# A selective state-space layer with a mixture of experts: nine row states in place of eight, three of the row products summed by accumulating DMAs, and a new order of work

## The reference

```python
proj = einsum('blh,he->bel', xn, W_in); hidden, gate = split(proj, 2)      # E = 512 channels each
hidden = silu(causal_conv4(hidden) + conv_bias)
dt, Bm, Cm = split(hidden^T @ W_x, [128, 144])                             # N = 16 states
dts = softplus(dt @ W_dt + b_dt); A = -exp(A_log)
state[n] = exp(dts * A[n]) * state[n] + dts * hidden * Bm[n]               # over the 256 tokens
scan_out = sum over n of state[n] * Cm[n]
ssm = ((scan_out + hidden * D) * silu(gate))^T @ W_out
# moe: softmax router over 32 experts, top 8 renormalised, sum of w_e * (silu(x@wg) * (x@wu)) @ wd, inner width 96
```

## Time and profile before

| | us |
|---|---|
| median of 3 runs | 1346.49 |
| runs | 1344.55 to 1347.49 |
| profiled execution, device time | 1342.44 |
| its span (first to last instruction) | 1340.6 |
| PE busy / PEld busy | 1301.6 / 1219.6 |
| DVE busy | 1239.6 |
| ACT busy | 1213.2 |
| POOL busy | 1233.9 |

### The profile page before, as it was taken

One profiled execution on the slowest core, in us unless ns is written; L12 is line 12 of the kernel. 1 busy time (PEld: TensorE's weight loads), 2 busy tenths in 40 slices (PEclk: granted clock), 3 DMA queues, 4 the chain that ended last, 5 costly groups with the idle time before them and its releaser, 6 DMA issues.

```text
span 1340.6 us, 26644 instructions
## 1 busy us (share of the span) xinstructions
PE 1301.6 (97%) x9222; PEld 1219.6 (91%) x9222; DVE 1239.6 (92%) x1644; ACT 1213.2 (90%) x2111; POOL 1233.9 (92%) x674
## 2 busy tenths in 40 slices
PE   6899999999999999999999999999999999999998
PEld 5889999999999999999999999999999899999987
DVE  3799999999999999999999999999999999999997
ACT  5879999999999999999999999999999899999984
POOL 2999999999999989999999999989999999999996
PEclk9999999999999999999999999999999999999999
DMA  7543443544444344443544444344443534434342
GB/s 193 160 144 118 143 120 115 152 115 132 139 127 135 112 136 127 139 120 118 149 120 126 136 128 138 114 132 131 139 122 116 148 114 134 139 113 142 109 146 80
DMA packets 189399, 174.95 MB, mean 130 GB/s; under 512 B 43185, under 2 KB 172241, under 8 KB 189265
## 3 DMA queue, kind: packets, MB, share of 16 engines
q1 hardware_dynamic: 150864, 121.86, 30.5%
q10 hardware_dynamic: 38400, 51.40, 13.6%
HBM read 167.92 MB, written 5.24 MB: 129 GB/s over the span
## 4 chain that ended last, share of the span: by engine, by line
POOL 27%; issue 21%; ACT 19%; DVE 18%; PE 12%; DMA 2%; ACTq 1%; SPq 0%; DVEq 0%; POOLq 0%
POOL state L571 14%; POOL moe L586 6%; ACT decay L657 5%; PE pair_ps L1003 5%; ACT L657 5%; ACT L665 4%; DVE state L878 4%; PE out_ps L1138 3%; POOL state L580 3%; DVE dt L865 3%; DVE u L891 2%; DVE decay L878 2%; DVE u L919 2%; ACT moe L665 2%; DVE moe L898 2%
## 5 line engine op out<-in xcount | busy, mean ns | idle before, releaser
L571 POOL TENSOR_TENSOR state<-du,b_rep 128x1024 f32<-128x1024 f32 x256 | 611.7, 2395 | 61.1 <-DVE u L891 59.3
L878 DVE TENSOR_TENSOR_SCAN state<-decay,state 128x512 f32<-128x512 f32 x448 | 534.2, 1212 | 21.1 <-ACT decay L657 16.4
L657 ACT ACTIVATE decay<-dt,neg_a 128x255 f32<-128x255 f32 x1024 | 436.7, 465 | 37.7 <-DVE state L878 19.0
L1138 PE MATMUL out_ps<-w_down,moe 128*128 128x256 f32 x1536 | 355.9, 381 | 3.1 <-POOL moe L586 1.9
L1138 PEld LDWEIGHTS out_ps<-w_down,moe 128*128 128x128 f32 x1536 | 282.5, 190 | 38.6 <-issue 4.1
L586 POOL TENSOR_TENSOR moe<-moe,rw_rep 128x512 f32<-128x512 f32 x192 | 249.3, 1309 | 8.7 <-DVE moe L898 7.3
L580 POOL TENSOR_TENSOR state<-state,c_rep 128x1024 f32<-128x1024 f32 x96 | 244.1, 2543 | 1.6 <-DVE state L878 1.6
L1003 PE MATMUL pair_ps<-xnT_hi,w_gate_hi 128*128 128x256 f32 x768 | 228.9, 298 | 3.2 <-DVE moe L898 3.2
L1003 PE MATMUL pair_ps<-xnT_hi,w_up_hi 128*128 128x256 f32 x768 | 225.7, 294 | 2.8 <-ACT moe L665 1.9
L657 ACT ACT_TABLE_LOAD x171 | 219.4, 1283 | 2.5
L1003 PE MATMUL pair_ps<-xnT_lo,w_gate_hi 128*128 128x256 f32 x768 | 216.4, 282 | 0.0
(11 more groups left out here) (149 smaller groups left out, 2252.5 us busy)
## 6 DMA issues: line engine op xcount, KB each, us to landing
w_down<-in_L_ffn_w_down_dram SPq DMA_DIRECT2D x384, 128.0 KB, 2.9
b_rep<-b_dram ACTq DMA_DIRECT2D x128, 256.0 KB, 3.3
rw_rep<-rw_dram SPq DMA_DIRECT2D x256, 96.0 KB, 2.7
c_rep<-b_dram ACTq DMA_DIRECT2D x128, 128.0 KB, 3.3
rw_rep<-rw_dram SPq DMA_DIRECT2D x256, 64.0 KB, 2.6
rw_rep<-rw_dram SPq DMA_DIRECT2D x256, 32.0 KB, 2.6
x_in<-L_attn_input_states_dram SPq DMA_DIRECT2D x16, 256.0 KB, 3.8
res<-L_attn_input_states_dram SPq DMA_DIRECT2D x16, 256.0 KB, 3.1
```

The lines of the kernel that those rows point to most:

```text
L571: pool.tensor_tensor(state[:, n % STATES, :, :], du2[:, q, :, :], b_rep[:, n // BCH % 2, n % BCH, :][:, None, :].broadcast_to([P, ET, T]), ...
L657: last = act.activation(decay[:, h, j, 1:T], dt[:, q, e, 1:T], ACT.Exp, scale=neg_a[:, e, n:n + 1])
L878: dve.tensor_tensor_scan(a if n in ROWS_BY_VECTOR else x, a, x, 0.0, ALU.mult, ALU.add).then_inc(scanned, 1)
L1138: last = pe.matmul(out_ps[:, c, :], moe[:, p % RING, j, c * P:(c + 1) * P], w_down[:, p % RING, j, :], start=(p == 0 and j == 0 and c == 0 ...
```

## The change

Row states are now (2, 4, 5, 6, 7, 9, 11, 12, 14). 5, 7 and 9 are VectorE's own; 2, 4, 6, 11, 12 and 14 are multiplied on GpSimd; of these, 11, 12 and 14 are added to `u2` not by VectorE but by a DMA that GpSimd issues with an add (`move_row`; 512 KB from SBUF to SBUF each). Seven states are left by turn. All tables of slots are new, those for the first and the last block too; ACT's table loads come out as 284 instead of 347, counted in the order of the two kernels.

```diff
-    BY_ROW = [n for n in range(NS) if n in ((2, 4, 5, 6, 8, 9, 10, 12))]
+    BY_ROW = [n for n in range(NS) if n in ((2, 4, 5, 6, 7, 9, 11, 12, 14))]
...
-    ROW_ADD_AT = [[42, 54, [45, 47], 70, 80, [76, 79], 106, 116], ...
+    ROW_ADD_AT = [[39, 53, [40, 46], 71, [61, 61], [75, 79], 93, 102, 118], ...
...
-    ROWS_BY_VECTOR = [n for n in BY_ROW if n in ((5, 9))]
+    ROWS_BY_VECTOR = [n for n in BY_ROW if n in ((5, 7, 9))]
+    ROWS_BY_DMA = [n for n in BY_ROW if n in ((11, 12, 14))]
...
+        def moved_at(i, n):
+
+            return (i * len(ROWS_BY_DMA) + ROWS_BY_DMA.index(n) + 1) * 16
...
+            elif ROW_SUMS[k] in ROWS_BY_DMA:
+                eng.wait_ge(row_moved, moved_at(i, ROW_SUMS[k]))
...
+                    elif before in ROWS_BY_DMA:
+                        pool.wait_ge(row_moved, moved_at(at, before))
...
+            def move_row(i, q, n):
+
+                wait_summed(pool, i, ROW_SUMS.index(n) - 1)
+                row_multiplied(pool, i, n)
+                pool.dma_start(u2[:, q, :, :], state[:, n % STATES, :, :], accum_op=ALU.add).then_inc(row_moved, 16)
...
             def gated(i, q):
 
+                pool.wait_ge(gate_read, 2 * i + 2)
                 pool.wait_ge(y_summed, 2 * i + 2)
...
+                for n, at in zip(BY_ROW, ROW_ADD_AT[s]):
+                    if n in ROWS_BY_DMA and a == at:
+                        move_row(i, q, n)
...
-                    if n not in ROWS_BY_VECTOR and a == at:
+                    if n not in ROWS_BY_VECTOR and n not in ROWS_BY_DMA and a == at:
                         add_row(i, q, n)
```

More of the change, by code:

```diff
@@ L102, in build @@
-    SCALAR_ALONE = [{'conv_silu': -74, 'router_exp': -94, 'softplus': -29, 'first_state': 4, 'skip': -9, 'normed': -123, 'share': -45},
-                    {'conv_silu': -73, 'router_exp': -84, 'softplus': -20, 'first_state': 7, 'skip': 23, 'normed': -122, 'share': -62},
-                    {'conv_silu': -73, 'router_exp': -77, 'softplus': -17, 'first_state': 13, 'skip': 4, 'normed': -123, 'share': -62}]
-    GATE_SILU_AT = [[54, 64], [63, 68], [74, 189]]
-    MUL_AT = [[-10, 13, 41, 55, 60, 67, 79, 85, 108, 112, 118, 124],
-              [14, 23, 41, 46, 59, 63, 79, 92, 107, 108, 127, 129],
-              [28, 34, 51, 54, 67, 72, 82, 82, 100, 117, 179, 190]]
@@ new lines, in build @@
+    OUT_AT = [[33, 43, 63, 71, 78, 84, 100, 119, 128, 128, 141, 141],
+              [39, 39, 57, 68, 70, 86, 103, 118, 118, 120, 141, 141],
+              [39, 65, 77, 108, 108, 174, 185, 188, 224, 235, 237, 253]]
+    TURN_AT = [[[8, 9], [9, 10], [22, 37], [74, 83], [103, 106], [122, 122], [130, 130]],
+               [[21, 22], [29, 29], [49, 49], [80, 82], [105, 105], [115, 116], [121, 129]],
+               [[14, 23], [24, 30], [37, 57], [84, 85], [154, 157], [182, 191], [211, 211]]]
+    TURN_Y_AT, PROJECT_AT = [[141, 141], [141, 142], [233, 233]], [163, 164, 254]
@@ new lines, in build @@
+    SCALAR_FRONT = [{'xnT': -116, 'hid0': -115, 'hid1': -114, 'weightsT': -6, 'low': -83, 'lowT': -82, 'dt0': -66, 'dt1': -51},
+                    {'xnT': -115, 'hid0': -102, 'hid1': -89, 'weightsT': -54, 'low': -44, 'lowT': -40, 'dt0': -30, 'dt1': -21},
+                    {'xnT': -110, 'hid0': -102, 'hid1': -90, 'weightsT': -49, 'low': -40, 'lowT': -33, 'dt0': -29, 'dt1': -22}]
+    SCALAR_ALONE = [{'conv_silu': -104, 'router_exp': -111, 'softplus': -24, 'first_state': 8, 'skip': 5, 'normed': -119, 'share': -93},
+                    {'conv_silu': -74, 'router_exp': -73, 'softplus': -17, 'first_state': 22, 'skip': 33, 'normed': -118, 'share': -60},
+                    {'conv_silu': -60, 'router_exp': -73, 'softplus': -18, 'first_state': 13, 'skip': 2, 'normed': -118, 'share': -59}]
@@ new lines, in build @@
+    GATE_SILU_AT = [[54, 71], [61, 71], [55, 151]]
+    MUL_AT = [[-22, -20, 30, 41, 56, 62, 77, 94, 108, 111, 128, 129],
+              [19, 31, 46, 48, 61, 63, 74, 77, 105, 109, 128, 130],
+              [18, 19, 47, 48, 66, 78, 93, 102, 124, 176, 213, 222]]
+    ADD_AT = [[[23, 30], [35, 68], [72, 97], [111, 114], [116, 126], [127, 132]],
+              [[28, 34], [69, 69], [92, 102], [105, 107], [118, 128], [128, 133]],
+              [[20, 29], [59, 61], [89, 89], [92, 119], [158, 170], [184, 209]]]
@@ new lines, in build @@
+    SUM_AT = [[136, 141], [141, 143], [240, 244]]
+    WEIGH_AT = [[19, 25, 29, 35, 51, 53, 84, 91, 101, 104, 122, 126],
+                [27, 30, 33, 41, 57, 65, 72, 85, 102, 105, 123, 124],
+                [26, 38, 51, 63, 63, 89, 97, 99, 131, 147, 237, 237]]
+    ROW_MUL_AT = [[21, 35, [40, 45], 51, [60, 61], [74, 79], 89, 100, 107], [21, 33, [44, 45], 45, [60, 62], [73, 76], 90, 95, 108], [20, 33, [43, 44], 55, [57, 62], [72, 78], 90, 125, 202]]
+    POOL_ALONE = [{'rstd': -103, 'step_input': -19, 'gated': 140, 'select': -47},
+                  {'rstd': -126, 'step_input': -22, 'gated': 139, 'select': -68},
+                  {'rstd': -122, 'step_input': -21, 'gated': 249, 'select': -60}]
@@ L138, in build @@
-    SPLIT_SCALAR_AT = [-115, -104, -102, -86, -73, -68, -51, -44, -41, -30, -28, -13, -7, -3, 0, 0, 10, 18]
-    SPLIT_POOL_AT = [-116, -112, -96, -69, -50, -2, 7, 11, 12]
+    WARM_AT = [[-73, 19], [8, 31], [22, 22]]
+    SPLIT_VECTOR_AT = [-108, -50, -50, -35, -34, -11, 6, 7, 16]
+    SPLIT_SCALAR_AT = [-121, -113, -112, -110, -88, -85, -83, -79, -50, -27, -23, -4, -4, -4, 1, 8, 8, 18]
+    SPLIT_POOL_AT = [-94, -25, -24, -21, -21, 5, 8, 9, 13]
     def pieces(p):
@@ L371, in row_at @@
         def row_at(i, n):
-            of = [k for k in BY_ROW if k not in ROWS_BY_VECTOR]
+            of = [k for k in BY_ROW if k not in ROWS_BY_VECTOR and k not in ROWS_BY_DMA]
             return i * len(of) + of.index(n) + 1
+        def moved_at(i, n):
+            return (i * len(ROWS_BY_DMA) + ROWS_BY_DMA.index(n) + 1) * 16
         def read_a(i, name):
```

54 lines of the change are left out of this document (16 added, 38 removed).

## The result

The changed kernel is slower: 1352.55 us (median of 5, 1351.1 to 1353.42) against 1345.43 us (median of 5, 1341.42 to 1347.49), a ratio of 1.0054 [1.0036, 1.0071]. The forecast was 1332.5, faster. Its direction was wrong. Its range, 1319 to 1358, held the time by luck: it reached that far up only for rival A, and what brought the time there was in good part the last block, which the forecast took to get 0.9 us shorter.

What follows compares the result with a forecast made beforehand. TensorE was taken as the bound; eight transposes fewer cut the period from 80.41 to 79.54 us, 13.9 us over 16 blocks: 1342.4 to 1328.5, plus 4.1 for the median, about 1332.5. The 80% range was 1319 to 1358.

Steps and rivals of the forecast that it cites:

- rival A: GpSimd becomes the bound through DMA issue and landing times; slower, 1368, at the upper ends 1403; chance 0.23.
- TensorE sets the pace, and the three others are close behind it.: Middle block: TensorE needs about 78 of 80.4 us, the largest need; DVE 3.5, POOL 4.8 and ACT 4.8 us away.
- buy nothing: VectorE, middle block: net -3.4 us, 76.85 to about 73.5, gains nothing by itself since VectorE isn't the bound.
- The 4.2 us of waiting for row adds are slack of an engine that is early: GpSimd's waits for VectorE's row adds, 4.2 us a block, were slack and counted as nothing.
- Behind the change no full add is left in that part: Where rows 10 and 12 were added, GpSimd's two lengthened operations lose their excess: 2.0 us, 75.6 to 73.6.
- c: Time one DMA issue holds GpSimd, put at 1.3 us between bounds 0.33 and 2.40; three with draining cost 4.2 us.
- The landing: Time until an adding DMA lands, put at 5 us; cost 0.2 us a block on GpSimd, ends 0 and 3.1.
- GpSimd's need: GpSimd's work and stalls in a middle block after the change: 78.0 us, 1.5 us under the forecast period of 79.54.
- The last landing is far from VectorE's `y_sum`: Block end: over 10 us of other work lie between, so the end of the block doesn't wait for it.
- C: Rival: half of TensorE's 2 us of stops a block also go, another 1.0 a block; time 1317, chance 0.15.
- rival B: No net gain: GpSimd's need between 79.5 and 80.4, or state 8's decays waiting for row 7; 1344 to 1349, chance 0.12.
- Start and last block, "unchanged": First and last block and the tables of the start were counted as unchanged.

Runs made afterwards that it cites:

- e1: Kernel before with 8 matmuls of pair 6's gate unit left out, 0.94 us less TensorE a block in its first half: 1345.65 us, ratio 1.0006.
- e5: Changed kernel with the same 8 matmuls of pair 6's gate unit left out, 0.94 us of TensorE a block: 1356.39 us, ratio 1.0095 to the kernel before.
- e11: Changed kernel without the three adding DMAs and their sums, and with 8 matmuls fewer a block: 1321.77 us, ratio 0.9837 to the kernel before.
- f1: Changed kernel with GpSimd's weight product of pair 9, late in the block, cut from 512 to 32 columns: 1342.56 us, ratio 0.9986 to the kernel before.
- e2: Changed kernel without the three adding DMAs and their sums; nobody waits for a landing: 1322.6 us, ratio 0.984 to the kernel before.
- f4: Kernel before with GpSimd's weight product of pair 9, late in the block, cut from 512 to 32 columns: 1338.38 us, ratio 0.996.
- e10: Changed kernel with pair 6's 8 matmuls left out and GpSimd's weight product of pair 6 cut to 32 columns: 1354.76 us, ratio 1.0085 to the kernel before.

## Why the prediction was wrong

**The step that failed: "TensorE sets the pace, and the three others are close behind it."** It was read off a budget over a whole block, 78 needed of 80.4. e1, e5 and e11 say no, in the kernel before, in the changed one, and without the DMAs: 0.94 us less of TensorE gave 0.07 us or nothing, cut in the first half. Every engine had 2 to 5 us of room over the block, and the period came from stretches in which one or two had none. (TensorE as one of several pacers late in a block of the kernel before is not excluded.) From this step it followed that VectorE's 4.5 us "buy nothing", that up to 1.5 us on GpSimd are free, and that the sum is the eight transposes. In its place the runs show that late in the block GpSimd counts (0.73 us of the period for 1.0 us of its work, f1), and there the DMAs stand: +2.03 us a block, against -1.91 for the rest of the change (e2, without three row sums). The forecast had 0 and -0.87.

**"The 4.2 us of waiting for row adds are slack of an engine that is early": wrong.** f4 takes one microsecond off GpSimd late in a block of the kernel before and shortens the period by 0.47. An engine can wait early in a block and be the pace late in it.

**"Behind the change no full add is left in that part": right, and only half of the matter.** GpSimd's long operations are gone (step input 3.34 to 2.64; adds on VectorE 1.55 us in the mean, now 1.24). But the three full adds that stay, and row 7, all lie in the first half, which they fill to 99%.

**The DMAs.** The issue was put at c = 1.3 with 0.1 for draining the product; it reads 0.94, of which 0.6 to 0.7 hold the queue, and the draining is 0.55. The reason given for the middle value, that GpSimd computes and ScalarE does not, is none: ScalarE is busy 75.6 us a block. Three cost 3.2 us of the queue instead of 4.2. The landing was put at 5: 5.4 in the median, with waits of 1.8 us in five blocks, 0.4 each instead of 0.2. GpSimd's need, forecast 78.0, is 77.45 busy and these waits. Between DMA 12 and the wait for its landing lie 8.2 us (682.60 to 690.82) and not over 9, which is still enough. All in all well sized, and compared with the wrong thing: a whole period instead of the second half. "The last landing is far from VectorE's `y_sum`" is right for the middle blocks and wrong for the last one, where `y_sum` stands 2.3 us for it.

**The others.** TensorE 79.94 to 78.92 a block (forecast -0.87), VectorE 76.85 to 72.35 (-3.4; the rest is the shorter adds), ScalarE 75.58 to 69.98 (forecast -4.4), table loads 284: right or nearly so as work, and without the effect on the period that C hoped for.

**The rivals.** Rival A named the mechanism, the DMAs' time on GpSimd, and the side. Its decision point was wrong: it asked for c over 2.1 us, since it too measured GpSimd against the whole block, and so its 1368 was too slow. The time of rival B, 1344 to 1349, was nearest, in the middle blocks above all, through a cause that it didn't name.

**Start and last block, "unchanged".** The first gate came 2.3 us later. Nothing is made of it, for with the order of the kernel before it came at 137.8 us in one trace (mean granted clock 0.99 up to there) and at 142.5 in another (e1, 0.95). Over all kernels here it came between 137.8 and 144.2. The last block's 5.9 us decide the direction: without them the kernel would lie 0.1% from the one before. Its order table was new, and the prediction only looked at the middle one.

**Open:** what exactly in the last block's table costs 3.1 us, and how much of it is the clock; why e5 and e10, with less to do, are slightly slower than the changed kernel (1.0095 and 1.0085, with intervals above or just touching its own; both traces have the same two long periods, the second, 82.5 and 82.1, and the fourth, 81.4 and 81.1); what TensorE's time is worth late in a block. None of the kernels that compute everything was faster than the kernel before.

## What to carry to other kernels

Where all engines are above 90%, cut the block's profile into stretches and ask for each which engine has no idle time in it; a mean over the block hides a load that is uneven, and moving work between engines moves it between stretches too. Check the pace with a cut of one microsecond in place, on the chip, before building on it: the same microsecond was worth 0.03 us in one half of the block and 0.73 in the other. A small share in the chain (12% TensorE in the kernel before) is a cheap first warning; a large one (35% after) proved nothing. When one operation too many costs more than its own length, look at TensorE's granted clock period by period.
